# 32x32 score tiles throughout, a new order of VectorE's work, earlier output turns and folded sums in a one-layer attention and mixing kernel

## What is computed

```python
# x: 16 batches of 256 tokens x 128; H = 16 heads of 8, KVH = 4 key heads
q, k, v = x @ Wq.T, x @ Wk.T, x @ Wv.T * sigmoid(x @ Wg.T)
q, k = rotate(rms_norm(q)) * q_gain, rotate(rms_norm(k))        # per head
q1, q2, k1, k2 = halves of each head (4 wide)                   # two attentions a head
a1 = softmax(causal(q1 @ k1.T / 2)) @ v;  a2 = softmax(causal(q2 @ k2.T / 2)) @ v
y = concat(a1 - lp * a2, a1 + lp * a2);  x1 = layernorm(x + y @ Wo.T)
gf = global_net(x1.mean(tokens))
out = x1
for _ in range(3):
    tf = coupling_net(out)                                      # 128-128-64-32-1, GELU
    out = out + (0.1 + adaptive_range * (0.7 * gf + 0.3 * tf - 0.5) * 2) * twist(out)
return layernorm(x1 + out)
```

## Time and profile before

| | |
|---|---|
| median of 3 runs | 266.91 us (266.88 to 267.43) |
| profiled execution | 267.33 us, span of its instructions 265.2 us |
| busy: PE, ACT, DVE, POOL | 245.1, 223.5, 195.3, 73.0 us |
| mean granted TensorE clock | 0.973 |
| exponentials of late, past, middle tiles (ACT) | 64, 64 and 16, 1.03 us each |

### The profile page before, as it was taken

One profiled execution on the slowest core, in us unless ns is written; L12 is line 12 of the kernel. 1 busy time (PEld: TensorE's weight loads), 2 busy tenths in 40 slices (PEclk: granted clock), 3 DMA queues, 4 the chain that ended last, 5 costly groups with the idle time before them and its releaser, 6 DMA issues.

```text
span 265.2 us, 9711 instructions
## 1 busy us (share of the span) xinstructions
PE 245.1 (92%) x3663; PEld 129.3 (49%) x3664; DVE 195.3 (74%) x747; ACT 223.5 (84%) x330; POOL 73.0 (28%) x193
## 2 busy tenths in 40 slices
PE   7369999999999999999999999898998999998980
PEld 4143554645646556465564554544643322223980
DVE  1879469797797887977969779652343877999992
ACT  3278989999999999999999999989874897777685
POOL 8630331423315223143132431402011000000473
PEclk9958999999999999999999999999999999999997
DMA  4304054251543515516245243451301356751045
GB/s 131 87 1 109 16 122 104 62 145 36 119 114 83 119 33 145 120 38 158 55 100 117 65 99 78 101 116 15 72 2 38 74 108 142 158 119 39 23 131 167
DMA packets 58218, 23.60 MB, mean 89 GB/s; under 512 B 42929, under 2 KB 56017, under 8 KB 58193
## 3 DMA queue, kind: packets, MB, share of 16 engines
q1 hardware_dynamic: 57904, 23.24, 36.9%
q10 hardware_dynamic: 288, 0.02, 0.1%
HBM read 5.04 MB, written 2.10 MB: 27 GB/s over the span
## 4 chain that ended last, share of the span: by engine, by line
PE 77%; DVE 7%; ACT 7%; issue 4%; DMA 2%; POOL 0%; ACTq 0%; DVEq 0%
PE O L629 11%; PE O L616 11%; PE S L749 9%; PE M L418 5%; PE S L512 5%; PE S L534 4%; PE S L502 4%; PE M L662 4%; PE M L648 3%; PE S L545 3%; PE S L554 2%; PE S L790 2%; PE O L636 2%; DMA qk<-parts 2%; PE S L759 2%
## 5 line engine op out<-in xcount | busy, mean ns | idle before, releaser
L927 ACT ACTIVATE probs_late<-S 128x1024 f32<-128x1024 f32 x64 | 63.4, 1029 | 1.0 <-PE S L534 0.9
L927 ACT ACTIVATE probs_past<-S 128x1024 f32<-128x1024 f32 x64 | 62.5, 1042 | 1.2 <-PE S L502 1.2
L616 PE MATMUL O<-probs_past,values 128*32 128x512 f32 x256 | 34.9, 618 | 1.4 <-ACT o_sb L933 1.3
L629 PE MATMUL O<-probs_late,mixed 128*32 128x128 f32 x512 | 26.5, 279 | 0.0
L1300 DVE TENSOR_TENSOR summed<-M,x_res 128x256 f32<-128x256 f32 x15 | 6.4, 425 | 26.9 <-PE M L662 26.9
L629 PE MATMUL O<-probs_late,values 128*32 128x128 f32 x512 | 25.7, 273 | 0.0
L1429 DVE SCALAR_TENSOR_TENSOR cY<-coup,ratio,Y 128x256 f32<-128x256 f32 x48 | 21.1, 481 | 5.9 <-ACT coup L1027 5.0
L1555 POOL TENSOR_TENSOR root_sq<-estimate 128x40 f32<-128x40 f32 x16 | 4.3, 266 | 76.5 <-DVE estimate L1180 72.3
L749 PE MATMUL S<-X,cn_w 128*128 128x512 f32 x48 | 25.0, 627 | 0.0
L512 PE MATMUL S<-qk 32*128 32x128 bf16 x512 | 19.0, 219 | 0.3 <-ACT probs_late L927 0.2
L512 PEld LDWEIGHTS S<-qk 32*128 32x128 bf16 x512 | 8.1, 92 | 20.8 <-issue 18.6
(11 more groups left out here) (190 smaller groups left out, 558.9 us busy)
## 6 DMA issues: line engine op xcount, KB each, us to landing
Y<-X SPq DMA_DIRECT2D x48, 128.0 KB, 2.4
xT_in<-in_xT SPq DMA_DIRECT2D x16, 128.0 KB, 2.8
x_res<-in_x SPq DMA_DIRECT2D x16, 128.0 KB, 2.1
out<-result SPq DMA_DIRECT2D x16, 128.0 KB, 1.9
future_in<-in_future SPq DMA_DIRECT2D x1, 256.0 KB, 2.9
qk<-parts SPq DMA_TRANSPOSE x15, 4.2
w_o<-in_w_o SPq DMA_DIRECT2D x2, 64.0 KB, 2.4
cn_w<-in_cn_w SPq DMA_DIRECT2D x2, 64.0 KB, 3.2
```

What stands on the lines that cost most here:

```text
L616: mm = pe.matmul(O[32 * g:32 * g + 32, :], values[p][:, 0, g, s, at:at + 32], probs_past[:, s, g, :], start=m == 0, stop=False)
L629: mm = pe.matmul(O[32 * g:32 * g + 32, :].rearrange("p (r n) -> p r n", r=R)[:, :, QUARTER * to:QUARTER * to + QUARTER], weights, probs_la ...
L927: act.activation(dst, S[TILE_BUFFER[n]][:, :, :], ACT.Exp).then_inc(exp_done[n], 1)
```

## The change

- Late tiles: `late_quarter` now makes 32x32 matmuls only, four key quarters a row, and takes in what `first_quarter` did; the mask is three triangles of 32 by 32 for each key group and half (`triangle`, `triangles`). Middle tiles likewise (`middle_part`, `middle_mask`). A late pair goes from 32 to 88 matmuls, a middle half from 10 to 20.
- PE's order: `turn_outputs` ahead of weigh(b, 1), `turn_x1` a batch later and behind `output_projection`, into the upper half of `M` (`X1_HALF`).
- `keep_x1` in the loop goes from ACT to DVE. ACT copies the projection before exponential 3, not behind it.
- DVE: squares, root and heads first, rotation behind them, `normalize_queries` ahead of `add_residual`, moments behind the split. `add_residual` waits for `turn_x1` too.
- The sum for the global net: POOL folds x1 of each batch to 64 columns (`fold_x1`), DVE sums eight batches at a time (`sum_x1(h)`), once in the tail and once in the first half cycle.
- PE's loop unrolls two batches more in front.

```diff
@@ -413,6 +416,7 @@
 
                 reach(pe, n_["qkvg_ready"], b)
                 reach(pe, n_["summed_done"], b - 3)
+                reach(pe, n_["X0_ready"], b - 4)
                 pe.wait_ge(xT_loaded[p], (half_b + 1) * 16)
...
@@ -507,52 +507,54 @@
                 _, s, h = TILES[n]
                 for t in range(T):
                     at = t * 256 + e * 128
+                    for c in range(4):
+                        first = e == 0 and c == (0 if t else 3)
+                        of = 1 - t if first else t
+                        keys = group_rows(c)
+                        for j in range(2):
+                            rows = group_rows(2 * h + j)
+                            q = qT[p][rows, of, :, s, keys] if first else quarters(p, rows, t, s)[:, 1 - e if t else 2 + e]
+                            pe.matmul(S[TILE_BUFFER[n]][keys, j, at:at + 128], kT[p][rows, of, s, keys], q,
+                                      start=e == 0 and t == 0, stop=False, skip_group_check=True)
+
+            def triangle(n, j, t, e, quadrant):
+
+                _, _, h = TILES[n]
+                g = 2 * h + j
+                at = t * 256 + e * 128
+                unit = ident16[group_rows(g), group_rows(g)].rearrange("p (o n) -> p o n", o=1).broadcast_to([QUARTER, R, QUARTER])
+                return pe.matmul(S[TILE_BUFFER[n]][group_rows(quadrant), j, at:at + 128], triangle16[group_rows(g), :],
+                                 unit, start=False, stop=True, skip_group_check=True)
+
+            def triangles(n):
+
+                for j in range(2):
+                    for t in range(T):
+                        triangle(n, j, t, 1, 0 if t else 3)
+                        triangle(n, j, t, 0, 1 if t else 2)
+                        mm = triangle(n, j, t, 0, 0 if t else 3)
+                mm.then_inc(scores_done[n], 1)
+
+            def middle_part(p, n, h):
+
+                for s in range(2):
+                    at = (2 * h + s) * 128
+                    for t in range(T):
+                        for c in (2 * t, 2 * t + 1):
+                            keys = group_rows(c)
+                            for j in range(2):
+                                rows = group_rows(2 * h + j)
+                                pe.matmul(S[TILE_BUFFER[n]][keys, j, at:at + 128], kT[p][rows, t, s, keys],
+                                          quarters(p, rows, t, s)[:, 1 + t], start=s == 0, stop=False, skip_group_check=True)
+
+            def middle_mask(n, h):
+
+                for t in range(T):
                     for j in range(2):
                         rows = group_rows(2 * h + j)
-                        pe.matmul(S[TILE_BUFFER[n]][:, j, at:at + 128], kT[p][rows, t, s, :],
-                                  quarters(p, rows, t, s)[:, 1 - e if t else 2 + e],
-                                  start=e == 0 and t == 0, stop=False, skip_group_check=True)
...
+                        unit = ident16[rows, rows].rearrange("p (o n) -> p o n", o=1).broadcast_to([QUARTER, 2 * R, QUARTER])
+                        mm = pe.matmul(S[TILE_BUFFER[n]][group_rows(1 + t), j, h * 256:(h + 1) * 256], triangle16[rows, :], unit,
                                        start=False, stop=True, skip_group_check=True)
-                mm.then_inc(scores_done[n], 1)
...
@@ -579,19 +581,18 @@
 
             def late_pair(b, p, n):
 
+                pe.wait_ge(n_["ident16_ready"], 2)
                 for m in (n, n + 1):
                     bank_free(b, m)
+                for e in range(2):
+                    for m in (n, n + 1):
+                        late_quarter(p, m, e)
                 for m in (n, n + 1):
-                    late_quarter(p, m, 0)
-                for m in (n, n + 1):
-                    first_quarter(p, m)
-                for m in (n, n + 1):
-                    late_quarter(p, m, 1)
-                for m in (n, n + 1):
...
-                weigh(b, p, 1)
-                if not first and not second:
-                    turn_x1(b - 2, project_more)
-                late_pair(b, p, 6)
                 if not first:
                     turn_outputs(b - 1, project_more)
+                weigh(b, p, 1)
+                late_pair(b, p, 6)
                 middle_half(b, p, 8, 0)
...
                 exponentials(b, 0)
                 exponentials(b, 1)
                 if not first:
                     copy_outputs(b - 1)
                 exponentials(b, 2)
-                exponentials(b, 3)
                 if project_more:
                     copy_projection(b + 2, p)
+                exponentials(b, 3)
                 exponentials(b, 4)
-                if not first and not second:
-                    keep_x1(b - 2)
                 exponentials(b, 5)
...
             def add_residual(b, p, half_b, bank=M):
                 dve.wait_ge(n_["projected"], b + 1)
+                reach(dve, n_["x1_turned"], b)
                 dve.wait_ge(res_loaded[p], (half_b + 1) * 16)
                 dve.tensor_tensor(summed[:, :, :].rearrange("p t d -> p (t d)"), bank[:, 0:T * 128],
                                   x_res[p][:, :, :].rearrange("p t d -> p (t d)"), ALU.add).then_inc(n_["summed_done"], 1)
+
+            def keep_x1(b):
+                at = b * SEQ
+                dve.wait_ge(n_["x1_turned"], b + 1)
+                dve.tensor_copy(X0[:, bass.ds(at, SEQ)], X1_HALF).then_inc(n_["X0_ready"], 1)
 
...
-            def sum_x1(b):
-                at = b * SEQ
-                reach_alone(dve, n_["X0_ready"], b + 1, n_["zeros_ready"])
-                dve.tensor_reduce(xsum[:, bass.ds(b, 1)], X0[:, bass.ds(at, SEQ)], AX.X, ALU.add).then_inc(n_["xsum_ready"], 1)
+            def sum_x1(h):
+
+                at = slice(8 * h, 8 * h + 8)
+                dve.wait_ge(n_["folded_done"], 16 * h + 16)
+                dve.tensor_reduce(xsum[:, at], folded[:, 8 * h * FOLD:8 * (h + 1) * FOLD].rearrange("p (b n) -> p b n", b=8), AX.X, ALU.add)\
+                   .then_inc(n_["xsum_ready"], 1)
...
                 project_more = not last and not (isinstance(b, int) and b == BATCH - 2)
+                if project_more:
+                    sum_of_squares(b + 2, p)
+                    first_bits(b + 2)
+                if not first:
+                    invert_sums(b - 1)
+                if project_more:
+                    step_bits(b + 2)
+                if not first:
+                    scale_heads(b - 1)
+                if project_more:
+                    first_estimate(b + 2)
+                    turn_by_angles(b + 2, p)
                 if not first and not second:
                     normalize(b - 2)
                 if project_more:
-                    rotate(b + 2, p)
-                if not first:
-                    normalize_heads(b - 1)
-                if not first and not second:
-                    sum_x1(b - 2)
+                    add_rotated(b + 2)
                 if not last:
                     gate_values(b + 1, 1 - p)
                     if general:
                         subtract_maximum(b + 1, 1 - p)
-                if not first:
-                    add_residual(b - 1, 1 - p, half_b - (1 - p))
                 if project_more:
                     normalize_queries(b + 2)
                 if not first:
-                    output_moments(b - 1)
+                    add_residual(b - 1, 1 - p, half_b - (1 - p))
+                if not first and not second:
+                    keep_x1(b - 2)
                 if project_more:
                     split(b + 2)
+                if not first:
+                    output_moments(b - 1)
 
             def output_weights():
 
...
@@ -1473,15 +1492,18 @@
 
             last_b = BATCH - 1
             coupling_gains()
+            sum_x1(0)
             normalize(last_b - 1)
-            normalize_heads(last_b, MB)
-            sum_x1(last_b - 1)
+            invert_sums(last_b, MB)
+            scale_heads(last_b, MB)
             add_residual(last_b, 1, BATCH // 2 - 1, MA)
             output_moments(last_b)
...
 
+            def fold_x1(b):
+
+                at = b * SEQ
+                pool.wait_ge(n_["X0_ready"], b + 1)
+                reach(pool, n_["folded_done"], b * 2)
+                pool.tensor_tensor(half_folded[:, :], X0[:, bass.ds(at, 128)], X0[:, bass.ds(at + 128, 128)], ALU.add)\
+                    .then_inc(n_["folded_done"], 1)
+                pool.wait_ge(n_["folded_done"], b * 2 + 1)
+                pool.tensor_tensor(folded[:, bass.ds(b * FOLD, FOLD)], half_folded[:, 0:FOLD], half_folded[:, FOLD:], ALU.add)\
+                    .then_inc(n_["folded_done"], 1)
+
```

More of the change, by code:

```diff
@@ L302, in block_kernel, with batches @@
         block = ctx.enter_context(nc.Block())
-        def batches(eng, step):
-            step(0, 0, 0)
-            step(1, 1, 0)
-            with eng.Fori(1, BATCH // 2 - 1) as i:
+        def batches(eng, step, apart=1):
+            for n in range(2 * apart):
```

(44 more changed lines are left out.)

80 lines of the change are left out of this document (25 added, 55 removed).

## The result

The changed kernel is slower: 286.6 us (284.9 to 289.8) against 267.1 us, ratio 1.071 (95% interval 1.065 to 1.077). The profiled execution took 285.87 us. Medians here are over all runs; the ratios leave out runs more than 1.5% above the fastest of the same kernel. The forecast of 254.0, its range to 264 and the sign were all wrong.

A forecast was written before the change was run, and what follows sets the result against it. PE was taken to bound the loop, ACT 6% behind; PE, ACT and hand-over sums of 9.9 to 10.06 gave 10.0 us a batch, 0.88 less. Batches saved 13.2 and 0.3, the tail cost 0.5: 254.0 us, range 250.5 to 264.

The forecast's parts named there:

- The late pair (1.4 us for two): PE's late score tiles: 0.6 us a pair, 0.7 with the switch, so 1.4 us a batch in place of 1.96.
- rival 1: Late pair no shorter than before, 0.9 to 1.1 us, as array tiles wait for each other; about 263 us; chance 0.21.
- rival 2: PE fed by number of instructions, small matmuls 15 to 31.6 ns apart; slower, up to about 328 us; chance 0.08.
- The middle tile (0.6): PE's middle score tile: both halves and a switch take 0.6 us a batch in place of 0.90.
- turn_x1 (0.28): On PE, moved behind the output projection of the same shape: 0.28 us in place of 0.37, one switch saved.
- The switch: PE's price for leaving a tile shape: 0.10 us, counted behind each late pair and once for the middle tile.
- Rival 3: Loop code no longer stays on PE, so four jumps back stall for fetches: +12 us, about 266 us; chance 0.05.
- The jump back: PE's return to the loop's start: fetch stalls only if the loop's code no longer fits, four jumps, +12 us.
- Its wait for the copy X: ACT's wait for PE before keep_x1's copy: 0.54 us a batch, to vanish with keep_x1 leaving ACT.
- DVE and POOL ("cost 0", "under 1 us"): DVE's added copy and moved wait cost nothing; POOL's two added sums take under 1 us a batch.
- The longest ring of hand-overs: Loop through ACT's exponentials and PE's scores, weighs and projection, back to o_sb's copy: 9.9 us a batch.
- Tail (+0.5): Kernel's end: turn_x1 on PE plus DVE's copy and sum, less the last xsum, add 0.5 us once.

The follow-up runs named there:

- e5: Changed kernel with the late pair's 88 matmuls reordered so its two tiles alternate after every eight matmuls; 286.8 us.
- e12: Kernel before with the replaced-quarter 32x32 matmuls repeated in the four straight-line batches, 128 more loads and matmuls a batch; 275.7 us, ratio 1.031.
- e4: Changed kernel with eight batches unrolled in front on PE in place of four; 295.7 us, ratio 1.109.
- e6: Kernel before with six batches unrolled in front on PE in place of two; 267.9 us, ratio 1.0011.
- e11: Changed kernel without 22 of the 24 triangle matmuls of a late pair, so only its times count; 272.4 us.
- e1: Changed kernel with the late and middle score tiles of before, everything else as changed; 266.43 us, ratio 0.9958.
- e10: e1 with the sum of x1 over batches 0 to 7 moved ahead of the residual of batch 14; 265.60 us, ratio 0.9933.
- e9: Changed kernel with the late tiles of before, only the middle tile in 32x32, and the sum over batches 0 to 7 earlier; 267.66 us, ratio 0.9994.
- e7: Changed kernel with a late pair of 56 matmuls: quarters in 32x128, then the replaced quarter and the triangles in 32x32; 275.9 us.

## Why the prediction was wrong

**The late pair (1.4 us for two).** The step that failed first. The text took "0.6 us, near the row of the same shape": L524's eight starts 3 to 4 ns apart. A pair measures 1.04 with its switch, not 0.70. The first 32 of the 88 do start within 0.15 us, but after a pause of 0.1 us the other quarters come 8.3 ns apart, whatever array tile they go to (e5, e12), and the 24 triangles take 0.38 us with a second pause of 0.1 in them. The size is that of rival 1, its mechanism isn't: it is rival 2's, PE fed by number of instructions, at 8.3 ns in place of the 15 to 31.6 that were weighed. From the first to the last of the 88 starts it is 0.89 us, 10 ns each, of the 12 at which rival 2 was said to decide. The 25 ns floor of the Trainium skill ("TensorE: Matmul & The Clock Gate", Part 1) doesn't hold for tiles of 32x32, which start 8.3 ns apart here. A short burst was extrapolated eightfold. Cost against the forecast: 0.67 us a batch.

**The middle tile (0.6), turn_x1 (0.28).** Right: 0.56 and 0.22. **The switch** (0.10) was not measured by itself.

**Instruction blocks.** Rival 3 had the right resource and the wrong place. It looked at the jump back, where the pass of some 1400 instructions did fit (no packet in q8 over four passes), and gave nothing to code executed once: six of sixteen batches straight-line and two in the loop's first pass. The row spoke of a jump, and no row was asked how often a block can come. 12.5 us. The unrolling of two batches more, listed in the change and priced at nothing, is part of it: e4 shows what each further batch costs, 2.3 us (9.1 for four); at the old density (e6) it costs nothing.

**The jump back.** Priced as a fetch or nothing. Before, PE still has 0.88 us of work ahead of the next past scores when the branch of 0.21 us begins (102.62 to 103.50); after, 0.28 us (117.46 to 117.74), and 0.3 us a pass shows. That PE's sequencer leads by a number of instructions, which small matmuls use up sooner, is the likely reading. 1.5 us in five passes.

**ACT.** Its wait for the copy X went, as said (exponential waits 0.56 us for L526 once a batch instead, because the pair comes late). PE bounds the loop, 21.16 of 21.37 us.

**DVE and POOL ("cost 0", "under 1 us").** Wrong, though hidden in the kernel as it is: DVE 17.86 of 22.00 becomes 19.11 of 21.37, POOL 6.80 becomes 9.98, 1.6 us more a batch. The longest ring of hand-overs was mis-sized too (e11).

**Tail (+0.5).** +6.2: two stops for blocks in it (0.78 and 1.28 us), then half the clock behind them (0.50 from 204.8 to 208.2 us), and the two sums in DVE's path. With the old tiles, without stops and without that stretch at half clock (e1), the same part still takes 87.2 us, 1.8 more than before. The chain of after there:

```profile
199.83 0.78 issue
...
203.36 1.28 issue
...
206.87 1.21 PE M L665 x4
...
211.04 0.68 DVE xsum L1332
...
225.96 0.69 DVE xsum L1332
```

L665 took 0.64 in the loop. The first sum was put at no more than twice 0.425 in the prediction and measures 0.68, of which the traces of e1 and e10 show 0.4 on the path. That the second stands before PE's global net (PE idle 1.31 us up to 226.8) was overlooked.

**The sum again.** 15 batches at 10.66 in place of 10.0: 9.9. Stops 12.5. Batch 1 waits for its transposing DMA, 2.0. Tail without stops, beyond the forecast: 3.6. The first six batches are another 3.2 longer than their stops and the mean period explain. Part of it is the clock: two of the three stretches at 0.50 lie in batches 1 and 5, whose mean clocks are 0.86 and 0.88 (before had 1.00 there). Of 3.4 us each, they can cost at most 1.7 us each, an estimate for a PE that is busy throughout. How much of the 3.2 they are was not measured. Together 31.2, where 285.87 - 254.3 = 31.6.

## What to carry over

Before splitting matmuls into smaller tiles, count instructions: here a load and matmul of 32x32 took 8.3 ns in a long run, so such a tile pays only where it replaces more array time than that. Count them twice where code runs once, in unrolled code and in a loop's first pass: at one block of 256 instructions in 5.9 or 6.6 us on average (e9, before) PE never stopped for code, at one in 4.7, 4.4 and 4.0 us (e7, e11, after) it did. And price a long run of instructions from a long run, or put down a gap of unknown size; a group of eight says nothing about eighty-eight.

## What was not expected of the hardware

A stop for code looks like idle time with the releaser "issue" in the middle of a group. It returns at multiples of 256 instructions and 2.2 to 3.1 us after a packet of a queue named instruction. The kernels that have many also scatter more from run to run, and some of their stops have a stretch at half clock behind them.

Some operations of DVE and POOL take longer where the two engines run together. In two loop batches of the kernel after (POOL, then DVE; mean ns, idle before):

```profile
L1577 POOL TENSOR_TENSOR root_sq<-estimate 128x40 f32<-128x40 f32 x2 | 0.9, 432 | 3.2 <-DVE estimate L1176 3.2
L1585 POOL TENSOR_TENSOR root_sq<-root_step,plus 128x40 f32<-128x40 f32 x3 | 1.6, 532 | 0.2
```

```profile
L1138 DVE TENSOR_TENSOR turned<-qkvg,rope_sin 128x160 f32<-128x160 f32 x4 | 1.4, 398 | 0.0
L1214 DVE CAST parts<-roped 128x128 bf16<-128x128 f32 x2 | 1.0, 480 | 0.0
```

Before, the same four operations took 252, 267, 316 and 220 ns. Now POOL's root runs beside DVE's rotation, and its fold of x1 beside the split. That the two engines hold each other up there is the likely reading and was not tried by itself. The Trainium skill ("GPSIMD Engine Reference", Specifications) says that GpSimd's SBUF interfaces are shared with VectorE, with contention where a VectorE instruction has two SBUF inputs or runs in a two-port mode; the multiply L1138 has two inputs; of the cast's mode no row tells.
